# Spreading a layernorm's mean and reciprocal deviation over partitions: matrix products with ones, or GpSimd transfers through DRAM

## What is computed

```python
def _layernorm(x, axis=-1, eps=1e-05):
    m = jnp.mean(x, axis=axis, keepdims=True)
    v = jnp.var(x, axis=axis, keepdims=True)
    return (x - m) / jnp.sqrt(v + eps)
...
    x = x + _L0_xattn_ref(_layernorm(x, axis=-1), ctx_4096, ctx_4096, mask, Wq, Wk, Wv, Wo)
    x = x + _L0_ffn_ref(_layernorm(x, axis=-1), W_base, b_base, W_router, A, B)
```

## Time and profile before

| | |
|---|---|
| Median of the runs | 2128.66 us (2127.95, 2128.66, 2129.84) |
| Profiled execution: its own time, its span | 2128.13 us, 2126.3 us |
| PE busy | 2118.6 us (100%) |
| DVE, ACT, POOL busy | 1652.2, 879.3, 338.8 us |
| Granted TensorE clock | 1.00 of full speed |
| DMA | 508.52 MB, mean 239 GB/s |

### The profile page before, as it was taken

The page is one execution under the profiler, slowest core; times in us unless marked ns, Lnnn a source line. Parts: engine busy times, 40 slices in busy tenths (PEclk is TensorE's granted clock), DMA queues, the critical chain, the costliest instruction groups (busy, mean ns, idle before and its releaser), DMA issues.

```text
span 2126.3 us, 26531 instructions
## 1 busy us (share of the span) xinstructions
PE 2118.6 (100%) x9429; PEld 1721.3 (81%) x9429; DVE 1652.2 (78%) x2387; ACT 879.3 (41%) x1353; POOL 338.8 (16%) x438
## 2 busy tenths in 40 slices
PE   9999999999999999999999999999999999999999
PEld 8888888888888888877777877777787777888887
DVE  6969759999986666677877888998999898856533
ACT  3323343222241111157555556655666566423211
POOL 0000025666350000003111111111111110100000
PEclk9999999999999999999999999999999999999999
DMA  8778667777685566679656666678557854596761
GB/s 314 244 247 287 237 208 303 277 282 267 258 320 210 211 216 212 219 249 314 226 190 197 232 238 198 198 257 290 199 171 264 295 197 153 191 359 247 283 248 61
DMA packets 198820, 508.52 MB, mean 239 GB/s; under 512 B 20896, under 2 KB 46624, under 8 KB 196640
## 3 DMA queue, kind: packets, MB, share of 16 engines
q1 hardware_dynamic: 172448, 424.43, 56.6%
q0 software_dynamic: 26240, 82.38, 11.6%
HBM read 357.26 MB, written 149.16 MB: 238 GB/s over the span
## 4 chain that ended last, share of the span: by engine, by line
PE 97%; DMA 1%; ACT 1%; DVE 0%; issue 0%; SPq 0%; ACTq 0%; DVEq 0%
PE pq L235 32%; PE pq L236 31%; PE pq L237 31%; PE pq L1300 1%; PE pq L1959 0%; PE pq L1958 0%; DMA raw<-gran 0%; DMA raw<-ctxT 0%; DMA RB<-rD 0%; DMA rD<-r 0%; PE pq L411 0%; ACT Rh L1225 0%; SPq L1122 0%; DVE Rl L1230 0%; ACT Pf L1439 0%
## 5 line engine op out<-in xcount | busy, mean ns | idle before, releaser
L235 PE MATMUL pq<-Ah,Rh 128*128 128x512 f32 x1024 | 399.0, 390 | 0.0
L237 PE MATMUL pq<-Ah,Rl 128*128 128x512 f32 x1024 | 398.5, 389 | 0.0
L236 PE MATMUL pq<-Al,Rh 128*128 128x512 f32 x1024 | 398.5, 389 | 0.0
L235 PE MATMUL pq<-Xq,qW 128*128 128x512 f32 x896 | 348.7, 389 | 0.5 <-issue 0.4
L236 PE MATMUL pq<-Xq,qW 128*128 128x512 f32 x896 | 348.6, 389 | 0.0
L237 PE MATMUL pq<-Xq,qW 128*128 128x512 f32 x896 | 348.5, 389 | 0.0
L1230 DVE TENSOR_TENSOR Rl<-raw,Rh 128x1024 fp32r<-128x1024 f32 x176 | 214.2, 1218 | 91.4 <-ACT Rh L1225 91.0
L1225 ACT ACTIVATE Rh<-raw 128x1024 fp32r<-128x1024 f32 x176 | 185.3, 1054 | 166.2 <-PE pq L237 128.2
L235 PEld LDWEIGHTS pq<-Ah,Rh 128*128 128x128 f32 x1024 | 192.2, 188 | 41.9 <-ACT Y L1451 0.8
L237 PEld LDWEIGHTS pq<-Ah,Rl 128*128 128x128 f32 x1024 | 192.2, 188 | 40.5
L236 PEld LDWEIGHTS pq<-Al,Rh 128*128 128x128 f32 x1024 | 192.2, 188 | 40.1
(11 more groups left out here) (243 smaller groups left out, 3935.2 us busy)
## 6 DMA issues: line engine op xcount, KB each, us to landing
raw<-gran SPq DMA_DIRECT2D x177, 512.0 KB, 4.4
QSD<-qW SPq DMA_DIRECT2D x64, 512.0 KB, 2.9
qD<-qt SPq DMA_DIRECT2D x128, 256.0 KB, 5.4
qW<-QSD SPq DMA_DIRECT2D x64, 512.0 KB, 3.4
qf<-qD SPq DMA_DIRECT2D x64, 512.0 KB, 6.1
RB<-rD POOLq DMA_DIRECT2D x128, 256.0 KB, 4.2
qraw<-gran SPq DMA_DIRECT2D x48, 512.0 KB, 5.2
kD<-kst SPq DMA_DIRECT2D x32, 512.0 KB, 5.7
```

The lines of the kernel that those rows point to most:

```text
L235: e.matmul(dst, lh, rh, start=first, stop=False, skip_group_check=more)
L236: e.matmul(dst, lh, rl, start=False, stop=False, skip_group_check=more)
L237: return e.matmul(dst, ll, rh, start=False, stop=last, skip_group_check=more)
```

## The change

`DIAG`, `SPREAD` and their three steps are taken out of `pe_kv`, `act_kv` and `dve_kv`. In their place POOL runs `rows_spread(t, c)` for each chunk: two transfers write the columns of `mv` (means, reciprocal deviations) as 4-byte elements to a row of 512 in DRAM (`rD`), and when each has landed a second transfer reads that row back into all 128 partitions of L or D. For chunks 0 and 1 this stands at the head of POOL's stream, for chunks 2 and 3 behind the last `XcD` store of the stage. The mean row is no longer negated, so the addition becomes a subtraction. Waits that had to do with the products go; those on the rows now wait for the transfers.

```diff
             for n in range(4, NK):
-                if n in SPREAD:
-                    c, i = SPREAD[n]
-                    whole, high, low = diagonal(c, i)
-                    t.wait_ge("kv_dgl", (c, i))
-                    if (c, i) in spread_before:
-                        t.wait_ge("kv_x", spread_before[c, i])
-                    elif c:
-                        t.wait_ge("kv_mask", 2)
-                    e.matmul(ps[7][:, :], ones[:, :], high[:, :], start=True, stop=False)
-                    e.matmul(ps[7][:, :], ones[:, :], low[:, :], start=False, stop=True).then_inc(*t.tick("kv_sp", (c, i)))
                 if n == MASK:
                     t.wait_ge("kv_mask", 1)
-                    t.wait_ge("kv_x", (1, 1))
...
         def act_kv(t):
-                if n in SPREAD:
-                    c, i = SPREAD[n]
-                    t.wait_ge("kv_sp", (c, i))
-                    if c > 1:
-                        t.wait_ge("kv_xn", (0, 3, c % 2))
-                    e.activation((xl0 if c % 2 == 0 else xl1)[i][:, :], ps[7][:, :], ACT.Copy,
-                                 scale=1.0 if i else -1.0).then_inc(*t.tick("kv_x", (c, i)))
...
-                if n - 1 in DIAG:
...
-                        e.activation(high[:, :], whole[:, :], ACT.Copy).then_inc(*t.tick("kv_dgh", (c, i)))
...
         def dve_kv(t):
-                if n in DIAG:
...
-                        e.tensor_tensor(v4(whole[:, :]), bc(ident.unsqueeze(1), [P, 4, P]), bc(mv[:, c, :, i:i + 1], [P, 4, P]),
-                                        ALU.mult).then_inc(*t.tick("kv_dg", (c, i)))
-                if n - 1 in DIAG:
...
-                        e.tensor_tensor(low[:, :], whole[:, :], f(high[:, :]), ALU.subtract).then_inc(*t.tick("kv_dgl", (c, i)))
...
-                        t.wait_ge("kv_x", (i, 0))
-                        e.tensor_tensor(y, y, m[:, :], ALU.add).then_inc(*t.tick("kv_xa", (0, k, i, kk // 4)))
+                        t.wait_ge(f"d_xl{i}0", i)
+                        e.tensor_tensor(y, y, m[:, :], ALU.subtract).then_inc(*t.tick("kv_xa", (0, k, i, kk // 4)))
...
+        def rows_spread(t, c):
+
+            e = t.e
+            t.wait_ge("kv_rs", (c, 5))
+            for i in range(2):
+                e.dma_start(rD[i, c, :].rearrange("(b p) -> p b", p=P), mv[:, c, :, i], allow_slow_non_contiguous=True).then_inc(
+                    *t.tick(f"d_mv{i}", c, 16))
+            if c > 1:
+                t.wait_ge("kv_xn", (0, 3, c % 2))
+            for i in range(2):
+                t.wait_ge(f"d_mv{i}", c)
+                e.dma_start((xl1 if c % 2 else xl0)[i][:, :], bc(rD[i, c:c + 1, :], [P, T])).then_inc(*t.tick(f"d_xl{c % 2}{i}", c, 16))
+
         def pool_kv(t):
             e = t.e
+            rows_spread(t, 0)
+            rows_spread(t, 1)
             for k, i in XBLOCK.values():
...
+            rows_spread(t, 2)
+            rows_spread(t, 3)
             for c, half, b4 in v_jobs:
```

More of the change, by code:

```diff
@@ L40 @@
     "low": ("kv_lo", "q_lo", "w_lo"), "high": ("kv_hi", "q_hi", "w_hi"), "rope": ("kv_rope", "q_rope"),
-    "prep": ("kv_dg", "kv_dgl", "kv_bn", "kv_rs", "kv_mask", "kv_xb", "set", "q_xl0", "q_xl2"), "kv_low": ("kv_kl", "kv_vl", "v_vl"),
-    "kv_high": ("kv_kh", "kv_vh", "v_vh"), "prep_act": ("kv_sq", "kv_dgh", "kv_x"), "p": ("a_exp", "a_ph"),
+    "prep": ("kv_bn", "kv_rs", "kv_mask", "kv_xb", "set", "q_xl0", "q_xl2"), "kv_low": ("kv_kl", "kv_vl", "v_vl"),
+    "kv_high": ("kv_kh", "kv_vh", "v_vh"), "prep_act": ("kv_sq",), "p": ("a_exp", "a_ph"),
     "top": ("f_lg", "f_m8", "f_ix", "f_pr", "f_ixf", "f_oh", "f_w", "f_wx", "f_r2"), "f_act": ("f_e", "f_h", "f_hwh"),
@@ L45 @@
     "xn": ("kv_xa", "kv_xm", "kv_xn"), "low_pool": ("q_lop", "q_xl1"), "job": ("kv_job", "q_pe", "v_job", "o_job", "f_job"),
-    "pe_prep": ("kv_vq", "kv_sp", "kv_mm"), "ln_dve": ("ln_v", "ln_xl", "ln_sum", "ln_sl", "ln_x", "ln_acc", "ln_r", "ln_u"), "f_hws": ("f_hw", "f_hwl"),
+    "pe_prep": ("kv_vq", "kv_mm"), "ln_dve": ("ln_v", "ln_xl", "ln_sum", "ln_sl", "ln_x", "ln_acc", "ln_r", "ln_u"), "f_hws": ("f_hw", "f_hwl"),
 }
@@ L58 @@
 SHARED_DMA += [(f"d_rb{i}", [f"d_bx{i}"]) for i in range(4)]
+SHARED_DMA += [(f"d_{x}{i}", [f"d_{y}{i}"]) for x, y in (("rt", "mv"), ("rs", "xl0"), ("x2", "xl1")) for i in range(2)]
 SHARED_DMA += [(f"d_x1{k}", [f"d_xt{k}"]) for k in range(4)]
@@ L613, in dve_kv @@
                         t.wait_ge(f"d_yx{i}{kk // 2}", 0)
-                        t.wait_ge("kv_x", (i, 0))
-                        e.tensor_tensor(y, y, m[:, :], ALU.add).then_inc(*t.tick("kv_xa", (0, k, i, kk // 4)))
+                        t.wait_ge(f"d_xl{i}0", i)
+                        e.tensor_tensor(y, y, m[:, :], ALU.subtract).then_inc(*t.tick("kv_xa", (0, k, i, kk // 4)))
                     for kk in (k, k + 4):
                         y = Yx[i][:, kk, :]
-                        t.wait_ge("kv_x", (i, 1))
+                        t.wait_ge(f"d_xl{i}1", i)
                         t.wait_ge("kv_xa", (0, k, i, kk // 4))
@@ L629, in dve_kv @@
                             t.wait_ge(f"d_xs{k % 2}{x}", (cp, k - 2))
-                    else:
-                        t.wait_ge("kv_sp", (2 * cp + 1, 1))
                     e.tensor_tensor(t1, b12, b11, ALU.subtract).then_inc(*t.tick("kv_xb", (cp, k, 0)))
@@ L763, in q_sum @@
             if n == 0:
-                t.wait_ge("kv_sp", (3, 1))
+                for i in (1, 3, 4, 5):
+                    t.wait_ge(f"d_xs1{i}", (0, 3))
             elif n < 15:
@@ L814, in x_block @@
                     t.wait_ge(f"d_bx{b}", k)
-                    t.wait_ge("kv_x", (3, 1))
-                    e.tensor_tensor(y, y, m[:, :], ALU.add).then_inc(*t.tick("q_xa", (k, b)))
+                    t.wait_ge(f"d_xl{b // 2}0", 2 + b // 2)
+                    e.tensor_tensor(y, y, m[:, :], ALU.subtract).then_inc(*t.tick("q_xa", (k, b)))
                 if what == "mult":
                     t.wait_ge("q_xa", (k, b))
+                    t.wait_ge(f"d_xl{b // 2}1", 2 + b // 2)
                     e.tensor_tensor(y, y, s[:, :], ALU.mult).then_inc(*t.tick("q_xm", (k, b)))
```

6 lines of the change are left out of this document (removed).

## The result

The changed kernel takes 2148.5 us in the median of 6 runs (2145.22 to 2158.96), the kernel before 2128.81 us (2127.95 to 2131.32) beside it. The ratio is 1.0099, with a 95% interval of 1.0076 to 1.0123: slower by 19.7 us, where 4.0 us less was forecast and 2123.0 to 2127.6 us was the range. Of all the runs in this document two lie far off the others, at 2646.46 us (the kernel before) and 3872.12 us (the late pair alone), and are left out of the ratios and of the late pair's median. The profiled execution took 2146.06 us with a span of 2144.2 us, 17.9 us more than the span before.

The account below looks back on a forecast made before the run. PE was taken to bound the kernel. Eight spreads at 0.50 us gave 4.0 us, all other terms 0, so 2128.66 - 4.0 = 2124.7 us, range 2123.0 to 2127.6 us.

Parts of the forecast that it names:

- What bounds the kernel: K/V stage: PE is never kept waiting, so what leaves its stream is gained; it carries 97% of the chain.
- Eight spreads at 0.50 us: PE in the K/V stage: eight spreads of two matmuls go, 0.50 us each, 4.0 us gained in all.
- DVE and ACT relieved, worth nothing: K/V stage: DVE and ACT lose 16 instructions each; PE waited for neither, so 0 us.
- The chain to L and D: POOL's stores and loads, chunks 0 and 1: L complete at 101.1 us, D at 110.8, before DVE reads them; price 0.
- D's margin of 18.8 us: Time between D's completion at 110.8 us and DVE's first read of it at 129.6 us.
- DMA load priced at 0, bound 3.5 us: Extra loads of 2.1 MB and stores of 16 KB; 3.5 us push near 187 to 205 us, against 6.8 us margin.
- The rival "slower": Rows come late, DVE stands still, PE waits for weights; 2137.6 us at a 45 us store landing; chance 0.07.
- a rival at 0.11 on the gaining side: Extra transfers in the densest stretch delay a weight or context piece by up to 3.5 us: 2126.4 to 2128.2 us; chance 0.11.
- The rule weighed: 4-byte stores: pieces under 512 bytes could land later than 7.1 us; forecast unchanged while landing stays below 7.1 + 18.6 us.

Follow-up runs that it names:

- the late pair alone: Chunks 2 and 3 stored to DRAM as in the change, chunks 0 and 1 gathered in SBUF: 2130.03 us, ratio 1.0008 to the kernel before.
- idle stores: Eight 4-byte-piece stores into a spare tensor nobody reads, added to the kernel gathering rows in SBUF (2124.33 us): side by side 2150.16 us, 512 bytes apart 2125.12.
- the first and fourth row of the table: Unread stores of 512 4-byte pieces added to the kernel gathering rows in SBUF: first, side by side, 2150.16 us; fourth, 512 bytes apart, 2125.12 us.

## Why the prediction was wrong

**What bounds the kernel**: right. PE never waits in the stage, and a wait that reaches PE costs its whole length. It costs more, in fact: 1.7 us for the lower clock behind the pauses of 2.9 and 13.6 us, a term that the prediction did not have.

**Eight spreads at 0.50 us**: right, measured directly. With the pieces in SBUF PE gains 2.0 us by 131 us and 4.0 us by 267 us, and the median falls by 4.7 us (2129.03 to 2124.33). What it falls by beyond 4.0 is not told apart from scatter: the profiled executions differ by 0.5 us the other way in the start-up already.

**DVE and ACT relieved, worth nothing**: right.

**The chain to L and D**: the landing of the 4-byte store was the mis-sized term, 15.8 us where 7.1 was taken. L was complete at 111.2 us and D at 129.9 us, not at 101.1 and 110.8. L's still was inside its margin. D's 129.9 us is on the edge of the 129.6 us needed, so this alone would have cost next to nothing, by the prediction's own count of what DVE and PE have in hand. DVE was by then so late by other causes that it waited for neither. The count had a gap all the same: it set a landing of 25.7 us (7.1 + 18.6) as harmless, and one of 32.1 us (7.1 + 25.0) as the first that PE feels, by L alone. D stands behind two such landings in a row, so each further microsecond of landing counts double there. By the prediction's own rows D's margin of 18.8 us is used up at a landing of 16.5 us, and PE stands still from about 18.7 us on (129.6 + 2.77 + 1.6 = 134.0 us for D).

**DMA load priced at 0, bound 3.5 us**: this is the step that failed. The stores were counted as "16 KB". Two of them are 1024 pieces, 64 for each of 16 DMA engines, and the pair takes 17 us the first time and 21 the second, 0.27 and 0.33 us a piece (an estimate from the landings, if all engines share alike). In that time all that moves is 51 GB/s where it was 246 (90 to 104 us), and 93 where it was 269 (108 to 125 us). The price is a K store of 24.6 us where none of the six before took over 7.5, a store buffer that ACT waits for, and everything in order behind it. The prediction looked for what might be pushed near 187 to 205 us, where the engines were 93% busy; it did not ask who shares the engines at 86 us, where the first stores run.

**The rival "slower"**: the right sign with the wrong mechanism. It priced a delay of the rows and needed a landing of 40.4 us (by the chain to D it would have been about 23); the loss came with a landing of 15.8 us, and comes even when no one waits for the store. The 0.07 for "slower" was the chance of one mechanism only. Contention among the DMA engines was a rival at 0.11 on the gaining side, limited by bytes. (Its heading has 1 to 3 us gained net; its own terms give 0.5 to 2.2.)

**The rule weighed.** The Trainium skill, "DMA: Bandwidth & Descriptors", section Specifications, says that below 512 bytes the DMA does a read-modify-write. The prediction asked only what that does to the landing of the store itself. The runs agree with it in part: packed 4-byte pieces are very slow. As a threshold for harm to other transfers 512 bytes does not hold here: 64-byte pieces, 16-byte pieces side by side and 4-byte pieces 16 bytes apart are all far under 512 bytes, and cost nothing measurable here. The same page, section "Why small descriptors are slow (HBM only)", says that transfers between SBUF and SBUF don't suffer the penalty; the kernel with its pieces in SBUF agrees, 5.5 us a landing, but does not single SBUF out, since pieces into DRAM land in 6.6 to 7.8 us when they are not packed 4-byte ones.

**What is shown and what is not.** Shown: the 4-byte stores into DRAM cause the loss (rows turned by PE, pieces in SBUF); it is crowding and not waiting (idle stores); 4-byte targets next to one another do it, and neither 512 pieces nor pieces of 4 bytes are enough by themselves (512 bytes apart), and the queue does not matter (issued by ACT). Not shown: why neighbours hurt. That each write reads back and rewrites a unit of memory that its neighbours are rewriting too would fit the first and fourth row of the table. But pieces 16 bytes apart, and pieces of 16 bytes side by side, would share any unit of 32 bytes or more with a neighbour as well, and are harmless. So either the unit is 16 bytes or less, or it takes more than a few writers to one unit; distances of 8 bytes, and pieces of 8, were not tried. The 16-byte pieces side by side were also a quarter in number, so that run alone does not tell size from number; and which DMA engines write the neighbours was not varied.

## What to carry to other kernels

Count a transfer by its pieces and by where they land, not by its bytes, and ask of a slow one who shares its DMA engines at that moment and which store buffer an in-order engine will not get back; 16 KB stored as 4-byte neighbours cost this kernel 24 us, 2 MB of broadcast loads nothing that shows. Where a column over partitions must become a row, collect it in one partition of SBUF first (or turn it on PE) and write it out whole: 2124.3 us here, against 2148.5 for the direct way. When a rival is slower by one mechanism, look for a second one that gets the same sign, since the chance of "slower" belongs to all of them.

## What the runs showed of the hardware

- Eight stores of 512 packed 4-byte pieces into DRAM, 16 KB in all, cost 24 to 26 us, with or without a reader. Their landing is 15.8 us from POOL's queue and 17.9 us from ACT's. Moved 16 bytes apart, they land in 7.8 us and cost about 1.4 us at most.
- Meanwhile, from 90 to 104 us, the DMA engines are nearly as busy as before (0.66 against 0.72) at 51 against 246 GB/s, and the busy time is booked on the held packets of the other queue (65.3%), not on those of the small stores (at most 0.6%). A high busy share of the DMA says nothing of the bytes; the two columns have to be read together.
- After pauses of 2.9 and 13.6 us, PE ran its next eight or so matmuls 0.43 us apart and not 0.23, at the lower granted level, for 1.7 us each time.
- The whole broadcast detour (2.1 MB of loads) cost nothing that the medians show: with the pieces in SBUF 4.7 us gained, against 4.0 for the spreads alone.
